# A cross-network tower with its layer-0 base rows read from SBUF, direct halves summed from PSUM, and sums kept in DRAM

## What is computed

```python
x0 = xk = e                                    # [2048, 39, 16]
for idx, (W, b) in enumerate(params):          # W: [39, k, 128], k = 39, 64, 64
    z = relu(einsum('bhd,bkd,hks->bsd', x0, xk, W) + b[None, :, None])
    if idx != 2:
        xk = z[:, :64, :]
        direct.append(z[:, 64:, :])
    else:
        direct.append(z)
logit = sum(concatenate(direct, axis=1), axis=-1)          # [2048, 256]
h = concatenate([logit, dense_ctx], axis=1)                # [2048, 272]
h = maximum(h @ W_top1 + b_top1, 0); h = maximum(h @ W_top2 + b_top2, 0)
y = h @ W_top3
```

## Time and profile before

| | us |
|---|---|
| median of 3 runs | 2551.4 |
| lowest and highest run | 2550.67 to 2551.43 |
| the profiled execution, own time | 2557.01 |
| its span, first to last instruction | 2555.3 |
| mean granted TensorE clock in it | 0.995 |

### The profile page before, as it was taken

The page is one execution under the profiler, slowest core; times in us unless marked ns, Lnnn a source line. Parts: engine busy times, 40 slices in busy tenths (PEclk is TensorE's granted clock), DMA queues, the critical chain, the costliest instruction groups (busy, mean ns, idle before and its releaser), DMA issues.

```text
span 2555.3 us, 25999 instructions
## 1 busy us (share of the span) xinstructions
PE 2434.8 (95%) x7712; PEld 1425.0 (56%) x7712; DVE 2269.2 (89%) x1356; ACT 1175.5 (46%) x1414; POOL 1558.9 (61%) x1030
## 2 busy tenths in 40 slices
PE   0499999999999999999999999999999999999999
PEld 0255555555555555555555565555555555555553
DVE  0499999999999999999999999999999999999960
ACT  0145444444444454544444444544444444445442
POOL 6466676666667666766666676667666666743240
PEclk9899999999999999999999999999999999999999
DMA  2977776877678687767867776777778677776610
GB/s 60 231 189 195 204 211 173 218 199 195 183 209 218 179 203 201 210 175 208 212 190 188 215 214 177 199 208 208 175 216 205 186 193 211 209 176 201 195 30 0
DMA packets 262599, 477.02 MB, mean 187 GB/s; under 512 B 19371, under 2 KB 37675, under 8 KB 262501
## 3 DMA queue, kind: packets, MB, share of 16 engines
q1 hardware_dynamic: 141622, 271.05, 39.4%
q10 hardware_dynamic: 100480, 200.29, 28.8%
q0 software_dynamic: 20480, 5.47, 1.4%
HBM read 468.99 MB, written 7.74 MB: 187 GB/s over the span
## 4 chain that ended last, share of the span: by engine, by line
PE 69%; POOL 11%; DVE 6%; issue 5%; DMA 5%; ACT 2%; another core or an unknown queue 1%; SPq 0%; POOLq 0%; DVEq 0%; ACTq 0%
PE z L686 35%; PE z L709 31%; POOL emb L345 6%; DVE prod L412 4%; POOL pair_lo L210 4%; DMA emb<-in_tbl,idx 4%; PE xk L768 1%; PE z L768 1%; ACT pair_hi L526 1%; POOL half_parts L206 1%; DVE logit L442 1%; DVE pair_lo L210 1%; PE turned L667 1%; DMA x_diag<-x_transposed 1%
## 5 line engine op out<-in xcount | busy, mean ns | idle before, releaser
L412 DVE TENSOR_TENSOR prod<-x_pairs,xk 128x2048 f32<-128x2048 f32 x640 | 1436.7, 2284 | 74.7 <-PE z L709 49.6
L686 PE MATMUL z<-prod,w_plain 128*128 128x512 f32 (+2 forms) x2944 | 1383.3, 594 | 41.8 <-issue 26.4
L526 ACT CAST pair_hi<-prod 128x1024 fp32r<-128x1024 f32 x703 | 735.6, 1046 | 1077.5 <-PE z L709 756.0
L210 POOL TENSOR_TENSOR pair_lo<-prod,pair_hi 128x1024 fp32r<-128x1024 f32 x320 | 764.0, 2387 | 641.9 <-ACT pair_hi L526 625.2
L686 PEld LDWEIGHTS z<-prod,w_plain 128*128 128x128 f32 (+2 forms) x2944 | 555.7, 189 | 475.5 <-issue 400.7
L345 POOL DMA_INDIRECT emb<-in_tbl,idx x624 | 701.5, 1124 | 189.4 <-issue 173.2
L709 PE MATMUL z<-pair_hi,w_lo 128*128 128x512 f32 (+1 forms) x1408 | 787.6, 559 | 2.3 <-DVE pair_lo L210 1.7
L709 PE MATMUL z<-pair_hi,w_hi 128*128 128x512 f32 (+1 forms) x1408 | 556.3, 395 | 0.0
L709 PE MATMUL z<-pair_lo,w_hi 128*128 128x512 f32 (+1 forms) x1408 | 555.5, 395 | 0.0
L210 DVE TENSOR_TENSOR pair_lo<-prod,pair_hi 128x1024 fp32r<-128x1024 f32 (+1 forms) x384 | 468.5, 1220 | 49.4 <-ACT pair_hi L526 49.4
L709 PEld LDWEIGHTS z<-pair_hi,w_lo 128*128 128x128 f32 (+1 forms) x1408 | 265.5, 189 | 297.3 <-POOL pair_lo L210 137.1
(11 more groups left out here) (50 smaller groups left out, 566.2 us busy)
## 6 DMA issues: line engine op xcount, KB each, us to landing
x_pairs<-x_transposed ACTq DMA_DIRECT2D x64, 2432.0 KB
x_pairs<-x_transposed SPq DMA_DIRECT2D x64, 2432.0 KB
x_diag<-x_transposed SPq DMA_DIRECT2D x128, 546.0 KB
x_diag<-x_transposed ACTq DMA_DIRECT2D x64, 546.0 KB
x_pairs<-x_transposed SPq DMA_DIRECT2D x64, 256.0 KB
emb<-in_tbl,idx POOLq DMA_INDIRECT x624
x_diag<-x_transposed SPq DMA_DIRECT2D x128, 78.0 KB
x_transposed<-stage SPq DMA_DIRECT2D x32, 156.0 KB
```

Source lines behind the costliest of these rows:

```text
L210: engine.tensor_tensor(pair_lo[0:rows, pair % PAIR_RING], held[0:rows, at:at + 2, :], pair_hi[0:rows, pair % PAIR_RING].bitcast(F32), ALU. ...
L412: nc.vector.tensor_tensor(prod[0:rows, pos % RING, 0:n, :], a, xk.unsqueeze(1).broadcast_to([rows, n, N]), ALU.mult).then_inc(prod_ready, 1)
L526: nc.scalar.copy(pair_hi[0:rows, pair % PAIR_RING], held[:, at:at + 2, :]).then_inc(hi_ready, 1)
L686: ins = nc.tensor.matmul(z[n][:], w, held[0:rows, i, :], start=(k == 0 and i == plain[0]), stop=(k == last_slot and not here and i == plai ...
```

## The change

1. **Base rows from SBUF.** `xk0` and ACT's copy into it go. The layer-0 products read both inputs from `x0_diag` in SBUF, and DVE waits for the load itself (`x0_diag_in`).
2. **Direct halves in PSUM.** `direct01` takes the PSUM bank of `xk0`, so that `sum01` reads PSUM.
3. **Sums of four chunks.** `sum01` and `sum2` write into windows of 128 columns. SP stores a window to DRAM once a group, and DVE waits for the store before it writes the window again. The top loads the columns of three quarters of the rows and 384 more from DRAM.
4. **Half tile's low on partitions 0 to 63**, in place of 64 to 127.
5. **Fewer landing waits.** POOL waits for landed gathers in c = 1 alone, where the indices are overwritten.

```diff
-TOP_DMAS = 6
+TOP_DMAS = 10
...
-        direct01 = sb("direct01", [P, N])
-        logit01 = sb("logit01", [P, B])
-        logit2 = sb("logit2", [P, CB + B])
+        logit01 = sb("logit01", [P, NB])
+        logit2 = sb("logit2", [P, NB])
...
+        early01, early2 = top_part(17, 3), top_part(13, 3)
+        window01, window2 = logit01[:, NB - P:], logit2[:, NB - P:]
...
-        xk0 = ps("xk0")
+        direct01 = ps("direct01")
...
-                engine.tensor_tensor(half_parts[HALF:P], held[HALF:P, at, :],
-                                     half_parts[HALF:P].bitcast(F32),
+                engine.tensor_tensor(half_parts[0:HALF], held[0:HALF, at, :],
+                                     half_parts[0:HALF].bitcast(F32),
...
+            def store_window(which, bt):
+
+                window, stored = ((window01, window01_stored), (window2, window2_stored))[which]
+                cols = sums[which, :, bass.ds(ahead(bt * P), P)]
+                sp.dma_start(cols, window).then_inc(stored, 16)
...
+                sp.wait_ge(window01_stored, 16 * GROUPS)
+                sp.wait_ge(window2_stored, 16 * GROUPS)
...
+                    (early01, sums[0, :, P:P + B - NB]), (early2, sums[1, :, P:P + B - NB]),
+                    (logit01[:, 0:NB - P], sums[0, :, P + B - NB:]),
+                    (logit2[:, 0:NB - P], sums[1, :, P + B - NB:]),
...
             def group(bt, last):
                 for c in range(CHUNKS):
+                    if c == 0:
+                        sp.wait_ge(summed01, bt * CHUNKS + 1)
+                        store_window(0, bt)
+                    if c == 1:
+                        sp.wait_ge(summed2, bt * CHUNKS + 2)
+                        store_window(1, bt)
...
-                    pool.wait_ge(gathered, 16 * ((bt + 1) * F + fields_done))
                     fields = fields_at[c]
                     if fields and fields[0] == 0:
+
+                        pool.wait_ge(gathered, 16 * (bt + 2) * F)
...
+            nc.vector.memset(window01, 0.0).then_inc(summed01, 1)
+            nc.vector.memset(window2, 0.0).then_inc(windows_zero, 1)
...
                     if n == k == 0:
-                        dve.wait_ge(xk0_ready, next_chunk + 1)
+                        dve.wait_ge(x0_diag_in, 16 * X0_DIAG_DMAS * (next_chunk + 1))
...
+                if c == 0:
+                    dve.wait_ge(window01_stored, 16 * (bt + 1))
+                nc.vector.tensor_reduce(window01[:, c * CB:(c + 1) * CB],
                                         direct01[:].rearrange("p (d b) -> p b d", b=CB),
...
+                if c == 1:
+                    dve.wait_ge(window2_stored, 16 * (bt + 1))
...
-                        steps += layer(0, x0_diag, xk0, slot + SLX, pos + SLX)
+                        steps += layer(0, x0_diag, x0_diag[:, T0, :], slot + SLX, pos + SLX)
...
-            def copy_xk0(chunk):
-                act.wait_ge(x0_diag_in, 16 * X0_DIAG_DMAS * (chunk + 1))
-                nc.scalar.copy(xk0[0:R0], x0_diag[0:R0, T0, :]).then_inc(xk0_ready, 1)
...
-                    terms = [(wt1a_sb[:, rows], logit01[:, n * NB:(n + 1) * NB]),
-                             (wt1b_sb[:, rows], logit2[:, CB + n * NB:CB + (n + 1) * NB]),
+                    of_chunk = (logit01, logit2) if n == B // NB - 1 else (
+                        early01[:, cols], early2[:, cols])
```

More of the change, by code:

```diff
@@ L160, in build @@
         turned = [ps("turned0"), ps("turned1")]
-        xk0 = ps("xk0")
+        direct01 = ps("direct01")
         xk1, xk2 = ps("xk1"), ps("xk2")
-        top = [z[0], z[1], xk0, xk1, xk2, z[2]]
+        top = [z[0], z[1], direct01, xk1, xk2, z[2]]
         swapped_in = sem("swapped_in")
@@ L194, in build @@
         summed2 = sem("summed2")
+        windows_zero = sem("windows_zero")
+        window01_stored = sem("window01_stored")
+        window2_stored = sem("window2_stored")
         h_ready = sem("h_ready")
@@ L437, in subtract, with sum01, sum2 @@
                 return split + 1, pair + (m == 2)
-            def sum01(chunk):
-                dve.wait_ge(direct01_ready, 2 * chunk + 2)
-                nc.vector.tensor_reduce(logit01[:, bass.ds(chunk * CB, CB)],
+            def sum01(bt, c):
+                dve.wait_ge(direct01_ready, 2 * (bt * CHUNKS + c) + 2)
+                if c == 0:
+                    dve.wait_ge(window01_stored, 16 * (bt + 1))
+                nc.vector.tensor_reduce(window01[:, c * CB:(c + 1) * CB],
                                         direct01[:].rearrange("p (d b) -> p b d", b=CB),
                                         AXIS.X, ALU.add).then_inc(summed01, 1)
-            def sum2(chunk):
-                dve.wait_ge(direct2_ready, chunk + 1)
-                nc.vector.tensor_reduce(logit2[:, bass.ds(chunk * CB, CB)],
+            def sum2(bt, c):
+                dve.wait_ge(direct2_ready, bt * CHUNKS + c + 1)
+                if c == 1:
+                    dve.wait_ge(window2_stored, 16 * (bt + 1))
+                at = (c + CHUNKS - 1) % CHUNKS * CB
+                nc.vector.tensor_reduce(window2[:, at:at + CB],
                                         z[2][:].rearrange("p (d b) -> p b d", b=CB),
@@ L454, in layer @@
                 return [(n, k, copies, xk, slot + k, pos + k) for k in range(SLX if n else SL0)]
-            products(layer(0, x0_diag, xk0, 0, 0), 0, 0, 0)
+            products(layer(0, x0_diag, x0_diag[:, T0, :], 0, 0), 0, 0, 0)
             nc.vector.memset(z[2][:], 0.0).then_inc(summed2, 1)
@@ L478, in group @@
                     slot, pos = slot + len(steps), pos + len(steps)
-                    sum2(chunk)
+                    sum2(bt, c)
                     dve.wait_ge(xk_ready[1], chunk + 1)
@@ L484, in group @@
                         if k == 1:
-                            sum01(chunk)
+                            sum01(bt, c)
                     pair = pair_after + PAIRS[2]
@@ L496, in _ @@
                 if n == 1:
-                    sum2(GROUPS * CHUNKS)
+                    sum2(GROUPS, 0)
                 dve.wait_ge(top_hi_ready, n + 2)
@@ L608, in group @@
                     direct_2(chunk, slot)
-                    if not (last and c == CHUNKS - 1):
-                        copy_xk0(chunk + 1)
                     pair = round_splits(SPLITS[1][EARLY[1]:], P, slot, pos, pair, held_by)
@@ L629, in group @@
                         hand_on(0, xk1, b0_sb, slot)
-                        act.wait_ge(summed01, chunk + 1)
+                        act.wait_ge(summed01, chunk + 2)
                         direct_0()
```

13 lines of the change are left out of this document (6 added, 7 removed).

## The result

The changed kernel takes **2686.9 us** (median of 4 runs, 2685.34 to 2689.16) against 2551.4 before: 1.0537 times as long, 95% interval 1.0525 to 1.055, 135.5 us lost where I had forecast 11 gained. Its profiled execution took 2685.34 us, with a span of 2683.6.

A forecast was written before the change was run, and what follows sets the result against it. PE, 95% busy, was taken as the bound, losing time to waits for POOL's low parts and the last gathers. Gains of 8.5 + 3 = 11.5 us from the median 2551.4 gave 2540, range 2534 to 2547 (8 in 10: 2531 to 2553).

The forecast's parts named there:

- Base rows from SBUF: Layer-0 products on DVE: unchanged in time, and the last gather gets in at the boundary behind the low part; 0 us.
- 0.2 us of room: Last gather of c = 0: asks at 1196.90, before DVE's low part ends at 1197.10, so it gets in there.
- The half tile's term: DVE's layer 1: 0.23 us less per chunk, so the last gather ends earlier and PE waits less; 3 us gained.
- the gather loses its place: Rival at the last gather: held through one layer-0 product, 2571, or all of DVE's layer 0, 2627; chance 0.15.
- the 8.5 of sum01: Layer 2 on DVE: sum01 from PSUM takes 0.38 us less, PE gets 0.18 in 47 chunks; 8.5 us gained.
- these zeros: Layer-0 products unchanged, and no waiting for window stores or x0_diag loads, which have time in hand; 0 us.
- the stall of ACT: At the start, ACT's `xk1` held 14.91 us; rival that this stall goes too, 6 us gained, 2534; chance 0.08.

The follow-up runs named there:

- e13_kinds: The changed kernel with an extra DVE operation ahead of the first layer-0 product: memset, copy and reduce in chunks 0, 1 and 2; 2696.8 us in one run.
- e1_half64_dve: The changed kernel with DVE's low part of the half tile back on partitions 64 to 127, POOL's staying on 0 to 63; 2538.6 us, ratio 0.9955.
- e18_drain_behind: The changed kernel with a VectorE wait for the half tile's low ahead of the product behind it, and POOL memsets ahead of the eighth gathers; 2530.9 us, ratio 0.9928.
- e5_base_only: The kernel before with one edit, the layer-0 base rows read from SBUF without ACT's copy; 2551.3 us, ratio 0.9994.
- e6_half0_only: The kernel before with one edit, the half tile's low on partitions 0 to 63 on DVE and POOL; 2554.2 us, ratio 1.0001.
- e4_seven: The changed kernel with 7 gathers in chunk 0 in place of 9; 2538.2 us, ratio 0.9942.

## Why the prediction was wrong

**The step that failed** is "Base rows from SBUF", where I put the term at 0. It rests on a model of a gather: it "needs, some 0.13 us after its start, something that DVE holds while both its inputs are in SBUF", and "it gets in at the boundary". In the changed kernel it still holds for one gather: the one at 1248.98 ends 0.81 after the end of the low part at 1249.95, though the next operation has two SBUF inputs as well. That low part stands ahead of the half tile's. The model is wrong for a gather that starts behind it, in the product ahead of the run. That product reads PSUM and by the model holds nothing; the gather asks at 1252.46, 0.2 us before the run, and should have been through. It took 8.52 us in place of 0.95, and PE's wait rose by 7.94 us a group. In `e13_kinds` the model is wrong inside of the run too: a gather passed three boundaries there without getting in at one. What it lacks: the boundaries inside of the run let a gather in only in the kernels where the product behind the half tile's low does not overlap it. I looked at the last gather and its "0.2 us of room". The one that was caught is the one before it, which the earlier trace rows don't even show; in the kernel before it lies across the start of the low part too (1195.52 to 1196.47) and takes 0.95 us. So the number that I watched, the room of the last gather, was not the number that decides.

**The two edits were priced one by one.** Alone each costs nothing (0.9994, 1.0001), and the prediction's sum would have stood. The half tile's term was told as 0.23 us of DVE's time, "it goes, and DVE gains". That the overlap itself, the very thing gained, changes whether a gather gets in, was in no term.

**The rival** "the gather loses its place" had the right outcome in its stronger form, a gather held for all of DVE's layer 0. It had another gather, the last, and another condition, the 0.2 us of room. Its price was 6 us a group and 2627. Measured are 7.6 us more for the gather (8.52 for 0.95) since the low part that opens the run counts too and the whole run goes by, not its rest, and 1.5 us of low clock behind PE's wait, which I had in no term., which spoke against it, show a gather among operations at the start, where no half tile's low stands; they could not speak for the new kernel.

**What was right.** Without the hold (`e1_half64_dve`) the change gives 2538.6 for a forecast of 2540, but in part by luck: the forecast has 3 us for the half tile, which this kernel lacks on DVE, and the 12 us measured have 4 of a shorter wait at the transposes. What is left, 8, is close to the 8.5 of sum01. In the changed kernel sum01 takes 684 ns (forecast 0.68), and the eight split matmuls of slot 2 take 1.87 (1.86), as the group of instructions and the chain in layer 2 of c = 2 show:

```profile
L466 DVE TENSOR_REDUCE logit<-direct 128x32 f32<-128x512 f32 x64 | 43.8, 684 | 0.0
```

```profile
1314.33 1.57 PE z L729 x6
...
1319.88 1.87 PE z L729 x8
...
1323.47 1.62 PE z L729 x6
```

PE's beat of layer 2 in the later chunks is 1.57 (slot 0), 1.87 (slot 2) and 1.62 (slot 3), against 1.60, 2.04 and 1.66 in the earlier trace rows: 0.24 us a chunk or 11 us for 47 chunks by this one chunk, where I had 0.18 and 8.5. The reduce from PSUM is as fast as the row said, and the 62 cycles more that the Trainium skill gives for PSUM ("VectorE: DVE Perf Modes", the section on the TRN2 errata) don't show in this strided read, 684 ns for 1060 from SBUF.

The half tile: the product follows 0.60 us behind it (forecast 0.60), and the low part ahead is 1.14 apart for 1.25. What that is worth in time no run shows: in after the hold covers it, and in `e18_drain_behind` the wait takes it back (1.14 + 0.80 = 1.94 us from the low part ahead to the product, for 1.25 + 0.72 = 1.97 before). So the term of 3 us stays untested. The layer-0 products are unchanged (2279 ns), PE, DVE and ACT never wait for a store, and DVE doesn't wait for the loads of `x0_diag` behind the start: these zeros hold.

The start: the stall of ACT in the earlier trace rows belonged to that one execution. PE's first transposes of the loop's groups stand at 166.39 there and at 159.96 in the profiled execution of `e5_base_only`, whose edit doesn't touch the start's loads. In `e6_half0_only`, whose only edit is the half tile's partitions, they stand at 158.56, and ACT's `xk1` at 95.26 in place of 104.63. That is more than the 5.6 us by which the profiled execution of before was over its median, so it was right to take it out by the median, and wrong to give it a rival.

## What to carry to other kernels

Where GpSimd issues gathers, list for each the VectorE operation under which it starts and the operations with two SBUF inputs behind it. Ask of an edit that closes a gap between VectorE operations which gathers come within the next microseconds: here a gap of 0.03 us, closed together with the base rows' move to SBUF, was worth 148 us. Price edits that meet on one engine together, not one by one. And a gather that must land for a critical step should not stand at the head of a long stretch of operations with two SBUF inputs; two gathers fewer ahead of that step took the whole loss away (`e4_seven`, 2538.2), though the holds in the other chunks stayed.

## What the runs showed of the hardware that I had not expected

- A gather can be held over five VectorE operations in a row, 7.35 us, and gets in only at the end of the last (8.52 us, in every chunk of the changed kernel). With the half tile on 64 to 127, gathers that start inside one of the same five get in at its end (`e5_base_only`: one that starts at 1190.36 in the low part of 1189.70 takes 1.38 us and ends 0.82 after that low part, though a product with two SBUF inputs has begun; another takes 1.90 in the product). With the half tile on 0 to 63 one that starts inside doesn't (`e13_kinds`, 6.43 us).
- The Trainium skill ("SBUF — State Buffer", "Who interferes with whom") says of VectorE's two-port modes that whoever issues first gets the shared ports for the whole instruction. The held eighth gathers started 0.12 to 0.43 us ahead of the low part and were held none the less, by it alone (2.38 us) or over the boundaries behind it (8.52).
- Whether a gather that starts in the product ahead of the run is held hangs on how that product began: overlapping the half tile's low ahead of it by 0.07 to 0.08 us, held at all distances met (0.12 to 0.43 us); 0.03 or 0.12 us after its end, never (0.17 to 0.59).
- Two VectorE operations overlap by 0.08 us when their operands start on the same partition and stand 0.03 us apart when they don't (1.25 and 0.72 us apart from start to start before, 1.14 and 0.60 after).
- In the 8.5 us without a matmul PE's granted clock was 1.00 up to 1264.0, 0.54 in the next 4 us, and 0.60 in the 4 us that follow, in which PE works again; after waits of 0.7 us the transposes took 1.09 us, at a clock of 1.00.
